# Score products of a gated cross-attention kernel: one float32 product or three float16 products

## The reference, cut to what matters

```python
x = x + tanh(g_xattn[0]) * xattn(layernorm(x), ctx, ctx, w_qs, w_ks, w_vs, w_proj, b_proj)
x = x + tanh(g_ffn[0])   * moe(layernorm(x), gate_w, w1, w2)        # 8 experts, top 2

def xattn(q, k, v, ...):                    # 4 x 1024 tokens of 256, 64 context rows, 16 heads of 64
    qh = einsum('bld,hdk->hblk', q, w_qs); kh, vh likewise from ctx
    attn = softmax(einsum('hblk,hbmk->hblm', qh, kh))      # the scores, changed here
    out = einsum('hblm,hbmk->hblk', attn, vh) * qh
    return heads_side_by_side(out) @ w_proj.T + b_proj
```

## Time and profile before

| | us |
|---|---|
| median of 3 executions (828.51 to 832.27) | 830.85 |
| the profiled execution | 832.27 |
| its span, first to last instruction | 830.5 |

### The profile page before, as it was taken

The page is one execution under the profiler, slowest core; times in us unless marked ns, Lnnn a source line. Parts: engine busy times, 40 slices in busy tenths (PEclk is TensorE's granted clock), DMA queues, the critical chain, the costliest instruction groups (busy, mean ns, idle before and its releaser), DMA issues. The chain is left out here.

```text
span 830.5 us, 23068 instructions
## 1 busy us (share of the span) xinstructions
PE 765.5 (92%) x7874; PEld 637.6 (77%) x7875; DVE 636.5 (77%) x1313; ACT 377.3 (45%) x687; POOL 403.6 (49%) x382
## 2 busy tenths in 40 slices
PE   3969999998999999998799999899999999999993
PEld 2647776666767666666589888799999999999993
DVE  7888999999999999999557667666666666666661
ACT  3565766665657666654234443233333323332331
POOL 4133544655656565656423485744444444444442
PEclk9999999999999999999899999999999999999998
DMA  8412241716345352613568774332233233322221
GB/s 273 158 50 103 83 147 63 250 71 222 109 145 178 107 171 79 222 46 140 167 193 238 200 215 119 72 59 44 44 51 51 44 48 47 51 45 50 46 34 20
DMA packets 48835, 92.50 MB, mean 111 GB/s; under 512 B 4921, under 2 KB 32578, under 8 KB 48770
## 3 DMA queue, kind: packets, MB, share of 16 engines
q1 hardware_dynamic: 25730, 64.78, 22.9%
q0 software_dynamic: 13392, 18.03, 12.3%
q10 hardware_dynamic: 9648, 8.85, 3.9%
HBM read 53.69 MB, written 37.95 MB: 110 GB/s over the span
## 5 line engine op out<-in xcount | busy, mean ns | idle before, releaser
L1391 PE MATMUL h_ps<-bx_h,w_now 128*128 128x128 f16 x2272 | 195.5, 220 | 0.5 <-DVE w_now L1527 0.5
L1404 PE MATMUL pair_ps<-weights,ht_h 128*128 x1136 | 190.4, 273 | 1.2 <-ACT y L1470 0.6
L1391 PE MATMUL h_ps<-bx_l,w_now 128*128 128x128 f16 x1136 | 156.8, 220 | 0.0
L1391 PEld LDWEIGHTS h_ps<-bx_h,w_now 128*128 128x128 f16 x2272 | 154.7, 98 | 1.7 <-issue 0.9
L1404 PE MATMUL pair_ps<-weights,ht_l 128*128 x568 | 154.8, 273 | 0.0
L1634 POOL TENSOR_TENSOR wait_mark<-wait_mark 128x1 f32<-128x1 f32 x71 | 46.9, 661 | 191.4 <-ACT y L1470 143.2
L1463 ACT ACTIVATE hid<-h_ps 128x1024 f32<-128x1024 f32 x71 | 72.7, 1024 | 142.8 <-PE h_ps L1391 142.8
L1205 POOL TENSOR_TENSOR r_l<-r,r_h 128x512 f16<-128x512 f32 x64 | 74.7, 1167 | 126.7 <-ACT r_h L799 122.4
L1635 POOL DMA_INDIRECT out<-y,meta x71 | 118.5, 1668 | 15.2 <-issue 7.8
L1533 DVE CAST ht_h<-hid 128x1024 f16<-128x1024 f32 x71 | 49.0, 691 | 100.1 <-ACT hid L1463 100.0
L1404 PEld LDWEIGHTS pair_ps<-weights,ht_h 128*128 128x128 f16 x1136 | 110.1, 97 | 16.0 <-issue 1.8
(11 more groups left out here) (266 smaller groups left out, 1442.9 us busy)
## 6 DMA issues: line engine op xcount, KB each, us to landing
stage<-in_w SPq DMA_DIRECT2D x16, 1024.0 KB, 7.6
w_split<-split SPq DMA_DIRECT2D x14, 1024.0 KB, 5.8
weights<-w_split SPq DMA_DIRECT2D x14, 1024.0 KB
rows<-records ACTq DMA_DIRECT2D x67, 129.0 KB, 2.1
xin<-in_x SPq DMA_DIRECT2D x8, 512.0 KB, 4.6
x_even<-in_x SPq DMA_DIRECT2D x4, 512.0 KB, 3.5
x_odd<-in_x SPq DMA_DIRECT2D x4, 512.0 KB, 3.4
out<-x_even SPq DMA_DIRECT2D x4, 512.0 KB, 2.7
```

What stands on the lines that cost most here:

```text
L1391: last = nc.tensor.matmul(h_ps[r % 2][:, c, :], w1_now[:, r % 2, s, k * F + c * P:k * F + c * P + P], xt[:, r % 2, k, :], start=(j == 0 an ...
L1404: last = nc.tensor.matmul(y_ps[r % 2], ht[:, r % 2, c, :], weights_at(e, s, WN // 2 + c * D, D).rearrange("p o n -> p (o n)"), start=(c == ...
```

## The change: what it does

The scores product takes float16 operands. `kb` becomes `kb_h` and `kb_l`; `q32` stays (for `times_q`), and `q_h` and `q_l`, two buffers each, are added beside it. Of each tile of 128 tokens PE does three float16 products in place of one float32 product. `q_h` is made by ACT, right behind the copy to `q32`, by a second pass over the same PSUM bank; `q_l` is made by POOL, between `normalize` and what follows it. `scores` waits for `q_lo`, `project_q` for `q_hi`. In group 0 `split_k` takes `place_k`'s place: ACT writes all four quarters of `kb_h` (64 x 128 each), then DVE all four of `kb_l` from PSUM and `kb_h`; `project_k`, the transposes of x and `scores` wait for DVE's part, `k_lo`.

```diff
         def project_q(g, p, par):
-            after(pe, q_sb, n - 1)
+            after(pe, q_hi, n - 1)
         def scores(b, n, p):
-            pe.wait_ge(q_sb, n + 1)
+            pe.wait_ge(q_lo, n + 1)
             if isinstance(n, int) and n < NP:
-                pe.wait_ge(k_placed, 2 * n + 2)
+                pe.wait_ge(k_lo, n + 1)
             after(pe, s_sub, n)
             for t in range(TG):
-                last = nc.tensor.matmul(s_ps[:, t]..., q32[:, p, t * P:(t + 1) * P], kb[:, b, p, :] ..., start=True, stop=True)
+                for i, (qt, kt) in enumerate(((q_h, kb_h), (q_h, kb_l), (q_l, kb_h))):
+                    last = nc.tensor.matmul(s_ps[:, t]..., qt[:, p % 2, t * P:(t + 1) * P], kt[:, b, p, :] ..., start=(i == 0), stop=(i == 2))
             last.then_inc(s_mm, 1)
@@ ACT
-        def place_k(p):
-            for d in range(2):
-                last = nc.scalar.copy(k_place(kb, p, 0, d), k_batches(0, d))
-            last.then_inc(k_placed, 1)
+        def split_k(p):
+            for h in range(2):
+                for d in range(2):
+                    last = nc.scalar.copy(k_place(kb_h, p, h, d), k_batches(h, d))
+            last.then_inc(k_hi, 1)
         def copy_q(n, p):
             nc.scalar.mul(q32[:, p, :], q_ps[p % 2][:, :], 1.0 / WS).then_inc(q_sb, 1)
+            after(act, s_mm, n - 1)
+            nc.scalar.mul(q_h[:, p % 2, :], q_ps[p % 2][:, :], 1.0 / WS).then_inc(q_hi, 1)
@@ DVE
-        nc.vector.memset(kb[:]....bitcast(U32), 0).then_inc(k_zeroed, 1)
+        for i, t in enumerate((kb_h, kb_l)):
+            nc.vector.memset(t[:]....bitcast(U32), 0).then_inc(k_zeroed, 1)
-        def place_k(p):
-            dve.wait_ge(k_mm, p + 1)
-            for d in range(2):
-                last = nc.vector.tensor_copy(k_place(kb, p, 1, d), k_batches(1, d))
-            last.then_inc(k_placed, 1)
+        def split_k(p):
+            dve.wait_ge(k_hi, p + 1)
+            for h in range(2):
+                for d in range(2):
+                    last = nc.vector.tensor_tensor(k_place(kb_l, p, h, d), k_batches(h, d), k_place(kb_h, p, h, d), ALU.subtract)
+            last.then_inc(k_lo, 1)
@@ POOL
+        def split_q(n, p):
+            pool.wait_ge(q_hi, n + 1)
+            nc.gpsimd.tensor_tensor(q_l[:, p % 2, :], q32[:, p, :], q_h[:, p % 2, :], ALU.subtract).then_inc(q_lo, 1)
         def step(g, k, p, pairs_back=LAST):
             if pairs_back >= 3:
                 normalize(n - 3, (p - 3) % NP)
+            split_q(n, p)
             if p == 3 and has_next(g):
                 ln_rstd(0, g + 1, ln1_ops, ln1_rstd)
```

More of the change, by code:

```diff
@@ L254, in attention @@
     wp_h, wp_l = (sb(f"wp_{s}", [P, NP, D], F16) for s in "hl")
-    kb = sb("kb", [P, B, NP, 2 * M], F32)
+    kb_h, kb_l = (sb(f"kb_{s}", [P, B, NP, 2 * M], F16) for s in "hl")
     vb_h, vb_l = (sb(f"vb_{s}", [P, B, NP, 2, DK], F16) for s in "hl")
@@ L277, in attention @@
     q32 = sb("q32", [P, NP, G], F32)
+    q_h, q_l = (sb(f"q_{s}", [P, 2, G], F16) for s in "hl")
     smax = sb("smax", [P, 2, TG, 2], F32)
@@ L331, in attention @@
         "ctx_tp", "ctx_copied", "gate_tp", "gate_copied", "wp_tp", "wp_hi", "wp_lo", "wq_hi", "wq_lo", "bias_hi"))
-    k_mm, k_placed, v_mm, v_hi, v_lo = (sem(n) for n in ("k_mm", "k_placed", "v_mm", "v_hi", "v_lo"))
+    k_mm, k_hi, k_lo, v_mm, v_hi, v_lo = (sem(n) for n in ("k_mm", "k_hi", "k_lo", "v_mm", "v_hi", "v_lo"))
     ln1_ops, ln1_rstd, ln1_shift, xn_done, xt_tp, xt_hi, xt_lo = (sem(n) for n in ("ln1_ops", "ln1_rstd", "ln1_shift", "xn_done", "xt_tp", "xt_hi", "xt_lo"))
-    q_mm, q_sb, s_mm, s_max, s_sub, e_x, pt_mm, e_hi, e_lo = (sem(n) for n in (
-        "q_mm", "q_sb", "s_mm", "s_max", "s_sub", "e_x", "pt_mm", "e_hi", "e_lo"))
+    q_mm, q_sb, q_hi, q_lo, s_mm, s_max, s_sub, e_x, pt_mm, e_hi, e_lo = (sem(n) for n in (
+        "q_mm", "q_sb", "q_hi", "q_lo", "s_mm", "s_max", "s_sub", "e_x", "pt_mm", "e_hi", "e_lo"))
     e_sum, e_inv, p_nrm, ot_mm, r_mul, r_hi, r_lo, pj_mm = (sem(n) for n in (
@@ L530, in project_k @@
             pe.wait_ge(wk_laid, 1)
-            after(pe, k_placed, 2 * p)
+            after(pe, k_lo, p)
             if p == 6:
@@ L566, in scores @@
         def scores(b, n, p):
-            pe.wait_ge(q_sb, n + 1)
+            pe.wait_ge(q_lo, n + 1)
             if isinstance(n, int) and n < NP:
-                pe.wait_ge(k_placed, 2 * n + 2)
+                pe.wait_ge(k_lo, n + 1)
             after(pe, s_sub, n)
             for t in range(TG):
[L572 to L575, removed]
+                for i, (qt, kt) in enumerate(((q_h, kb_h), (q_h, kb_l), (q_l, kb_h))):
+                    last = nc.tensor.matmul(s_ps[:, t].rearrange("p h m -> p (h m)"), qt[:, p % 2, t * P:(t + 1) * P],
+                                            kt[:, b, p, :] if isinstance(b, int)
+                                            else kt[:, bass.ds(b, 1), p, :].rearrange("p o m -> p (o m)"),
+                                            start=(i == 0), stop=(i == 2))
             last.then_inc(s_mm, 1)
@@ L652, in small_job @@
                 elif g == 0:
-                    pe.wait_ge(k_placed, 2 * p + 2)
+                    pe.wait_ge(k_lo, p + 1)
                 x_transpose(g + 1, 0, job_ps)
@@ L751, in _ @@
         nc.scalar.mul(bias_rows[:, 0, :], bias_sb[:, :], WS).then_inc(bias_hi, 1)
-        def place_k(p):
+        def split_k(p):
             act.wait_ge(k_mm, p + 1)
             if p == 0:
-                act.wait_ge(k_zeroed, 1)
-            for d in range(2):
-                last = nc.scalar.copy(k_place(kb, p, 0, d), k_batches(0, d))
-            last.then_inc(k_placed, 1)
+                act.wait_ge(k_zeroed, 2)
+            for h in range(2):
+                for d in range(2):
+                    last = nc.scalar.copy(k_place(kb_h, p, h, d), k_batches(h, d))
+            last.then_inc(k_hi, 1)
         def split_v(part):
@@ L843, in step @@
             if first:
-                place_k(p)
+                split_k(p)
             if p == 2 and known(g, 2):
@@ L896, in _ @@
     def _(dve):
-        nc.vector.memset(kb[:].rearrange("p b n m -> p (b n m)").bitcast(U32), 0).then_inc(k_zeroed, 1)
+        for i, t in enumerate((kb_h, kb_l)):
+            nc.vector.memset(t[:].rearrange("p b n m -> p (b n m)").bitcast(U32), 0).then_inc(k_zeroed, 1)
         nc.vector.memset(seen[:, :], 0.0)
@@ L952, in _ @@
                                        ALU.mult, ALU.subtract).then_inc(bias_hi, 1)
-        def place_k(p):
-            dve.wait_ge(k_mm, p + 1)
-            if p == 0:
-                dve.wait_ge(k_zeroed, 1)
-            for d in range(2):
-                last = nc.vector.tensor_copy(k_place(kb, p, 1, d), k_batches(1, d))
-            last.then_inc(k_placed, 1)
+        def split_k(p):
[4 more added lines that the diff above has]
+            last.then_inc(k_lo, 1)
         def split_v(part):
```

## The result

| | before | after |
|---|---|---|
| median of the timed executions, us (lowest to highest, how many) | 829.68 (828.25 to 832.27, 4: the three above and one more) | 850.59 (848.83 to 853.76, 4) |
| the profiled execution, its span | 832.27, 830.5 | 850.42, 848.8 |
| first product of the expert stage | 406.10 | 430.69 |

The change makes the kernel slower: ratio 1.0254, 95% interval 1.0225 to 1.0284, 20.9 us by the medians. 20.2 had been forecast, 852.5 us for the profiled execution and 851 for the median.

The account below looks back on a forecast made before the run. DVE was taken to bound attention's groups 2 to 7 (96% busy), PE running ahead. Terms -1 (PE), +1.4 (ACT), +16.5 (POOL's lock) and +3.3 (group 0) sum to +20.2 us: 852.5 us profiled, median 851, range 836 to 866.

Parts of the forecast that it names:

- p = 3: From group 3: `split_q` takes the root's place and holds L196 0.7 us longer in four groups, +2.8 us.
- group 0: `split_k` makes DVE wait for ACT: +2.1, +0.9 and +0.3 us in p = 5, 6 and 7, sum +3.3.
- p = 4, six groups: `split_q` right behind `pn` holds DVE's L194 0.9 us longer, 0.7 in one group: +5.2 us.
- p = 5, six groups: The first L217 gets in when `pn` ends, the second waits out `split_q`, +1.1 us each: +6.6 us.
- p = 7, groups 1 to 6: L1023 starts before `split_q` ends, +0.15 us in each of six groups: +0.9 us.
- ACT's pass and the steps of 4 us: ACT's extra pass delays DVE in tight steps, +1.4 us; `split_q` delays L1034 in short steps, +1.0.
- PE's credit: Shorter score products, 0.22 us a pair, 14 us over 64 pairs, credited only -1 us.
- It isn't waited for: PE's gain in the pair loop isn't waited for: DVE has 2.5 us of waits in 268.
- The lock: DVE instructions reading two SBUF inputs wait out POOL's elementwise `split_q`: +16.5 us; the no-lock rival, 836 us, chance 0.11.
- The step named, p = 5: In group 0, ACT held by `ln1_apply` makes DVE's key subtractions end at 48.7 us, not 46.6: +2.1.
- no term: TensorE's clock, at 1.00 from 107 to 375 us, given no cost: if it fell, PE had time to lose.
- The row beat the rule: Trace: the root holds no DVE instruction, +0; skill's rule: it holds L199, 4 us more, 856.5 us, chance 0.10.

Follow-up runs that it names:

- 3: Kernel before plus ACT's `q_h` and POOL's `split_q`, scores waiting for `q_lo` but still float32, keys placed as before: 846.88 us, ratio 1.0206.
- 5: Changed kernel with group 0's keys placed as before, half each by ACT and DVE, low part of keys left out: 844.26 us, ratio 1.0163.
- 1: Changed kernel with POOL's subtraction cut to 4 of 512 columns, all waits kept: 833.57 us, ratio 1.0063.
- 2: Changed kernel with the 4-column subtraction and a POOL memset of the other columns behind it: 835.90 us, ratio 1.0082.
- 7: Changed kernel, `split_q` later in p = 3, 4, 5 of groups 2 to 7, POOL waiting in p = 4 for DVE's choice: 833.29 us, ratio 1.0049.
- 11: Kernel before, unchanged, executed once more: 827.02 us, a single execution.
- 8: Kernel before, float32 scores, DVE's moments, choice and slots moved between `probs_lo` and `times_q`: 818.85 us, ratio 0.9865.
- run 4: Kernel before plus ACT's pass for `q_h`, used by nobody, `project_q` waiting for it: 832.05 us, a single execution.
- 10: Changed kernel's float16 products with the 4-column subtraction and DVE's short instructions moved between `probs_lo` and `times_q`: 822.62 us, ratio 0.9900.
- 6: Changed kernel with `split_q` later in POOL's list in p = 3, 4, 5 of groups 2 to 7, without an added wait: 845.36 us, ratio 1.0202.

## Why the prediction was right

The mechanism, its places and the total were right. That the total came so close is partly luck: attention ended 24.6 us later for 20.2, since the terms of p = 3 and of group 0 were too small, and the expert stage, which had been taken as unchanged, took 6.3 us less in the trace after than in the one before. Measured as longer steps, over groups 2 to 7 where nothing else is said:

| step of the prediction | forecast us | measured us |
|---|---|---|
| p = 4, six groups | +5.2 | +5.8 (0.88 in four, 1.62, 0.70) |
| p = 5, six groups | +6.6 | +6.1 (1.00 to 1.02 each) |
| p = 3 | +2.8 (four groups) | +5.0 (0.82 in four, 0.03, 1.67) |
| p = 7, groups 1 to 6 | +0.9 | about +0.5 (0.08 to 0.12 in five) |
| ACT's pass and the steps of 4 us | +2.4 | +1.8 (p = 0 1.3, the rest in p = 1, 6 and 7 of group 7 and p = 3 of group 1) |
| PE's credit | -1 | -0.9 (-0.39 in p = 2 of group 7, -0.52 in p = 5 of group 1) |
| group 0 | +3.3 | +6.3 (1.25 ahead of it, 0.26 in p = 3 and 4, 2.44, 1.93, 0.40) |
| not forecast: p = 4 of group 1, p = 7 of group 3 | | +0.70, -0.49 |
| to the end of attention | +20.2 | +24.6 |

- That DVE bounds the stage and PE's gain is worth little: shown by 3, whose float32 products leave the steps of groups 2 to 6 as long. The credit itself was even smaller than in the table: p = 5 of group 1 is 0.31 us shorter with float32 products too, and in group 7 p = 3 took back more than p = 2 gave. "It isn't waited for" doesn't hold in group 0, where 5 shows 0.22 us a pair in p = 3 and p = 4. DVE's waits before were 2.7 us and not 2.5: the view of the earlier trace rows has a third, of 0.2 us, for L189.
- The lock: shown by 1 (the length of the subtraction), 2 (reading, not being busy) and 7 (its place). That the first L217 gets in when `pn` ends and the second meets `split_q` came out to 0.1 us, 2.11 for 2.2.
- p = 3 was mis-sized: two groups of six should have escaped; one did, one took 1.67 us. There, and in p = 4 of group 6, DVE's instruction waits through two or three POOL instructions, and the chain starts right behind a scatter. The kernel after, group 6, DVE and then POOL:

```profile
334.15 2.85 DVE L926 SCALAR_TENSOR_TENSOR shift<-mv,rstd 128x4 f32<-128x4 f32 x1
...
332.63 1.04 POOL L1225 DMA_INDIRECT records<-rec_odd,slot_odd  x1 [0.20 <-issue]
333.70 1.17 POOL L1215 TENSOR_TENSOR r_l<-r,r_h 128x512 f16<-128x512 f32 x1
334.82 1.05 POOL L1209 TENSOR_TENSOR pn<-ex,rinv 128x512 f32<-128x512 f32 x1
335.82 1.15 POOL L1203 TENSOR_TENSOR q_l<-q,q_h 128x512 f16<-128x512 f32 x1
```

  Why DVE doesn't get in between here, as L193 and L194 do above, is open; 7 shows only what readiness behind a scatter does.
- Group 0 was mis-sized: 3.3 for 6.3. The step named, p = 5, was right, +2.44 for 2.1, with DVE waiting for ACT as drawn:

```profile
48.58 0.99 DVE L965 TENSOR_TENSOR kb_l<-job_ps,kb_h 64x128 f16<-64x128 f32 x4 [1.02 <-ACT kb_h L762]
```

  p = 6 brought 1.93 for 0.9. But the other parts can't all be laid to the change. The first sum of exponentials came 1.25 us later (35.96 for 34.71), and in the five traces with float32 scores and the keys placed as before it comes anywhere from 34.52 (11) to 35.78 (8). And I had given TensorE's clock no term. In the kernel after it was granted at 0.88 in this stretch, before at 0.96 over 23 to 66 us: PE waited 3.29 us for `xt_l` up to 67.39, and its products of 69.2 to 70.5 us come 0.107 us apart, at the 1.2 GHz level, where at 75.7 they come 0.056 apart. Run 7 has the same code in group 0 and p = 7 took 9.55 us there, not 10.50. Busy time and clock in p = 7, the kernel after, then run 7:

```profile
66.90:73.60 6.70, 6.21 (x28) 4.55 (x29) 3.50 (x9) 2.83 (x8) 2.03 (x2) 0.50 0.16 64
...
66.90:73.60 6.70, 6.30 (x56) 4.93 (x57) 4.45 (x11) 3.60 (x10) 1.93 (x2) 1.00 0.13 54
```

  In run 4, with the keys placed as before, p = 6 is 1.0 us longer and p = 7 1.55 shorter than before, with the clock at 0.50 from 52.9 to 59.7 us instead of 61.3 to 64.7. How much of the 6.3 is the hand-over from ACT to DVE and how much the clock stays open.
- The clock in groups 2 to 7: "no term" was right. It fell to 0.50 for a stretch in p = 4 of groups 2, 4, 6 and 7, and groups 2 and 4 are no longer for it than 3 and 5 in p = 4 and p = 5.
- The root didn't hold L199: it took 0.19 us inside `rstd` in all four groups. The row beat the rule, as forecast.
- The passage: attention ends 24.6 us later, the program 18.3 in the two traces, 20.9 by the medians. The profiled execution of before had the longest expert stage of all (424.4; 419.5 when taken again), which accounts for the traces' difference from the medians; the five kernels with the whole `split_q` beside float16 scores took 417.8 to 419.2, the eight others 419.5 to 424.4. Whether that is more than chance stays open.

## What to carry to other kernels

When an engine is full, ask which of its instructions end together with another engine's: DVE's short instructions waited out the long reading POOL instructions beside them, and reordering DVE's list took 11 us off the kernel before. An instruction given to an idle engine is free only if its port is; put it where the busy engine works from PSUM, and hold it back with a wait until then, but not so long that its result comes late. A shorter job on an engine that nobody waits for is worth nothing, and taking the bound away from one engine may uncover a third (by PE's waits ACT, in 10), not the one that was sped up.

## What the runs showed of the hardware

- POOL's elementwise instructions on 512 columns (`pn`, `r_l`, `q_l`, 1.03 to 1.17 us), which read SBUF, held DVE's short instructions on two SBUF inputs until 0.05 us after their end, and L213, on one, until 0.02 after. A POOL memset (0.94 us), a scatter with nothing ready behind it, and the root of 4 columns (1.04 us, though it reads SBUF) didn't; whether the root's few columns or its operation makes the difference isn't shown.
- Ready behind a running scatter, the reading instruction holds DVE before it starts: 1.89 us instead of 0.19 (6), gone with one wait (7).
- Three float16 products of 128x128 took 0.67 us for four tiles, one float32 product 0.89.
- At the granted clock of 0.50 twelve such float16 products took 1.28 us (69.23 to 70.51, group 0 of the kernel after).
- Taking DVE's short instructions out of that lock took 11 us of 830 off the kernel before (8); that isn't the lock's whole cost, since DVE waits 12.1 us for scores there.
